# First network of a two layer transformer: two buffers for the transposed input, the next batch turned ahead of the sixth gate and up pair, and sums awaited bank by bank

## The reference

```
logits = x @ W_router                                   # 8 experts
scores = sigmoid(logits); top 2 of scores + expert_bias, their scores normalised -> w
gate   = x @ W_gate + lora(x, sA_gate, sB_gate) + sum_e w_e * lora(x, A_gate[e], B_gate[e])
up     = x @ W_up   + lora(x, sA_up,   sB_up)   + sum_e w_e * lora(x, A_up[e],   B_up[e])
hidden = silu(gate) * up                                # 688 columns
out    = hidden @ W_down + lora(hidden, sA_down, sB_down) + sum_e w_e * lora(hidden, A_down[e], B_down[e])
```

## Time and profile before

| | |
|---|---|
| time, median of 3 runs | 1555.84 us (1554.02 to 1556.76) |
| profiled execution, time | 1562.64 us |
| profiled execution, span | 1560.8 us |
| PE busy | 1425.5 us, 91% of the span |
| DVE, ACT, POOL busy | 60%, 37%, 35% |
| granted TensorE clock, mean | 0.960 |
| first network, from the first turn of `x1` to the last sum | 655.5 to 871.1 us |

### The profile page before, as it was taken

How to read it: one execution, slowest core, us unless ns; L and a number is a source line. 1 busy time by engine, 2 the same in 40 slices (tenths; PEclk the granted TensorE clock), 3 DMA queues, 4 the chain that set the end, 5 groups by cost and what they waited for, 6 DMA issues and landing times.

```text
span 1560.8 us, 23982 instructions
## 1 busy us (share of the span) xinstructions
PE 1425.5 (91%) x8106; PEld 1133.1 (73%) x8106; DVE 941.5 (60%) x2170; ACT 569.9 (37%) x1441; POOL 553.6 (35%) x483
## 2 busy tenths in 40 slices
PE   7999999999999999899999699999999999575990
PEld 6777777777777777677676588788788788563650
DVE  4677777777777778534332456565665657464214
ACT  4444444444444444521211243333334333331320
POOL 3555555555555555001002213513532522103223
PEclk9999999999999999989989899999999999788996
DMA  5000000000002000200000020200200004925984
GB/s 172 1 11 1 11 0 10 7 3 7 3 7 63 0 0 1 74 7 0 1 0 0 0 75 8 62 22 14 68 7 13 7 15 124 280 95 158 275 232 121
DMA packets 68218, 76.35 MB, mean 49 GB/s; under 512 B 14205, under 2 KB 55445, under 8 KB 68149
## 3 DMA queue, kind: packets, MB, share of 16 engines
q1 hardware_dynamic: 56789, 58.49, 13.2%
q10 hardware_dynamic: 8288, 12.22, 2.6%
q0 software_dynamic: 3072, 4.72, 1.6%
HBM read 66.22 MB, written 9.21 MB: 48 GB/s over the span
## 4 chain that ended last, share of the span: by engine, by line
PE 81%; DVE 8%; POOL 3%; issue 3%; DMA 2%; ACT 2%; another core or an unknown queue 1%; POOLq 0%; ACTq 0%; DVEq 0%
PE ps L1612 39%; PE ps L1728 9%; PE ps L1713 7%; PE ps L1701 5%; PE ps L1758 4%; PE ps L1848 4%; PE ps L1706 2%; PE ps L2054 2%; PE ps L1925 1%; PE ps L2119 1%; PE ps L1915 1%; DMA sums_dram<-rows 1%; PE ps L2136 1%; PE ps L1730 1%; PE ps L1703 1%
## 5 line engine op out<-in xcount | busy, mean ns | idle before, releaser
L617 POOL TENSOR_TENSOR qk<-q,ksb 128x512 f32<-128x512 f32 x64 | 82.6, 1291 | 303.6 <-ACT q L841 214.2
L756 ACT ACTIVATE probs<-ps,nm 128x128 f32<-128x128 f32 (+3 forms) x256 | 134.0, 526 | 152.7 <-DVE nm L1116 152.7
L1728 PE MATMUL ps<-kT,qT 128*128 128x128 f32 (+3 forms) x512 | 174.6, 450 | 4.4 <-ACT probs L756 3.7
L1040 DVE TENSOR_TENSOR pT_low<-ps,pT 128x384 fp32r<-128x384 f32 (+2 forms) x256 | 99.7, 451 | 122.6 <-ACT pT L699 121.1
L1057 DVE TENSOR_TENSOR prod<-ps,rope_sb 128x1024 f32<-128x1024 f32 x128 | 150.2, 1215 | 6.4 <-PE ps L1612 6.4
L495 POOL TENSOR_TENSOR qT<-prod 64x512 f32<-64x512 f32 x64 | 81.3, 1270 | 170.2 <-DVE prod L1057 131.6
L699 ACT ACTIVATE pT<-ps 128x384 fp32r<-128x384 f32 (+2 forms) x256 | 84.9, 415 | 152.0 <-PE ps L1758 152.0
L1713 PE MATMUL ps<-U,oT 128*128 (+1 forms) x512 | 124.6, 386 | 0.7 <-ACT oT L699 0.7
L1116 DVE TENSOR_REDUCE nm<-ps 128x1 f32<-128x128 f32 (+3 forms) x256 | 113.7, 484 | 12.1 <-PE ps L1730 12.1
L495 POOL TENSOR_TENSOR kT<-prod 64x512 f32<-64x512 f32 x64 | 81.4, 1272 | 111.2 <-DVE prod L1057 108.7
L1166 DVE SCALAR_TENSOR_TENSOR acc<-ps,rinv,acc 128x256 f32<-128x256 f32 x256 | 109.5, 479 | 13.5 <-PE ps L1713 11.9
(11 more groups left out here) (256 smaller groups left out, 2763.1 us busy)
## 6 DMA issues: line engine op xcount, KB each, us to landing
eg<-in_L_ffn_w_gate_dram SPq DMA_DIRECT2D x16, 704.0 KB
eg<-in_L_ffn_w_up_dram SPq DMA_DIRECT2D x16, 704.0 KB
ed<-in_L_ffn_w_down_dram ACTq DMA_DIRECT2D x10, 640.0 KB
ksb<-ks_dram SPq DMA_DIRECT2D x16, 256.0 KB, 3.3
ed<-in_L_ffn_w_down_dram SPq DMA_DIRECT2D x6, 640.0 KB
rows_dram<-rows ACTq DMA_DIRECT2D x4, 640.0 KB, 3.3
acc<-in_L_attn_x_dram SPq DMA_DIRECT2D x4, 512.0 KB
wq_in<-in_L_attn_wq_dram SPq DMA_DIRECT2D x8, 256.0 KB, 2.8
```

The costliest lines, as they stand in the source:

```text
L617: nc.gpsimd.tensor_tensor(qk[:], q3[:], ksb[b % 2][:], ALU.mult).then_inc(qk_ready, 1)
L756: nc.scalar.activation(probs[hh][:, off:off + (i + 1) * P], ps[:, BS + i % 2, 0:(i + 1) * P], ACT.Exp, bias=nm[:, hh, i:i + 1], accum_out= ...
L1040: return nc.vector.tensor_tensor(o, whole, hi.bitcast(F32), ALU.subtract)
L1728: pe.matmul(ps[:, bank, 0:(i + 1) * P], qT[:, hh, b, i * P:(i + 1) * P], kT[:, hh, b, 0:(i + 1) * P], start=True, stop=False)
```

## The change

- `x1T` becomes two pairs of tiles, at 56 and at 102 KB of each partition; batch b uses pair `b % 2`.
- On PE, `turn_x1(b + 1)` is issued after the fifth pair (m = 4) and ahead of the sixth. `first_products(b + 1)` stays behind the sixth. On ACT `x1_halves(b + 1)` stands between the silus of m = 4 and m = 5, on DVE `x1_rests(b + 1)` between the products of m = 4 and m = 5.
- At the start of batch b, `base` waits ahead of each of its first four pieces for the sum of its own bank, in the order bank 0, 2, 1, 3 (the first, third, second and fourth sum), where it waited once for all four.
- The loops over batches are written out on PE, ACT and DVE (the tiles are chosen by `b % 2`); the constant `LINKS0` and the bookkeeping for the loop go.

```
--- before.py
+++ after.py
@@ -46,7 +46,6 @@
 PPC = 4
 BLOCKS = CHUNKS * BATCH
 
-LINKS0 = 39
 SCALE = float(DH) ** -0.5
 MASKED = -1.0e30
 ROPE_BASE = 10000.0
@@ -127,7 +126,7 @@
         gu = [place(f"gu{h}", 20 + 11 * h, [P, KD, 2, F0], F32R) for h in range(2)]
         lb = [place(f"lb{h}", 42 + 5.5 * h, [NL, 2, F0], F32R) for h in range(2)]
         la = [place(f"la{h}", 53 + 1.25 * h, [P, KD, NA], F32R) for h in range(2)]
-        x1T = [place(f"x1T{h}", 56 + 4 * h, [P, KD, T], F32R) for h in range(2)]
+        x1T = [[place(f"x1T{i}{h}", at + 4 * h, [P, KD, T], F32R) for h in range(2)] for i, at in enumerate((56, 102))]
         xaT = [place(f"xaT{h}", 64 + 4 * h, [NL, 2, T], F32R) for h in range(2)]
         gated = [place(f"gated{h}", 72 + 2 * h, [M0, T]) for h in range(2)]
         hidT = place("hidT", 76, [M0, FT0, T])
@@ -799,7 +798,7 @@
             def x1_halves(b):
                 for k in range(KD):
                     act.wait_ge(x1_turned, b * KD + (k + 1))
-                    copy(x1T[0][:, k, :], ps[:, 4 + k, :]).then_inc(x1hi_ready, 1)
+                    copy(x1T[b % 2][0][:, k, :], ps[:, 4 + k, :]).then_inc(x1hi_ready, 1)
 
             def scores0(b):
                 act.wait_ge(logits_ready, b + 1)
@@ -819,8 +818,9 @@
                     if m >= 2:
                         act.wait_ge(hid_ready, b * FT0 + (m - 1))
                     nc.scalar.activation(gated[m % 2][0:size, :], ps[0:size, m % 2, :], ACT.Silu).then_inc(gated_ready, 1)
+                    if m == 4 and not last:
+                        x1_halves(b + 1)
                 if not last:
-                    x1_halves(b + 1)
                     scores0(b + 1)
                     xa_halves(b + 1)
                 act.wait_ge(ha_turned, b + 1)
@@ -832,9 +832,8 @@
             x1_halves(0)
             scores0(0)
             xa_halves(0)
-            with act.Fori(0, BATCH - 1) as b:
-                ffn0(b, False)
-            ffn0(BATCH - 1, True)
+            for b in range(BATCH):
+                ffn0(b, b == BATCH - 1)
 
 
             def relu(o, i):
@@ -1191,7 +1190,7 @@
             def x1_rests(b):
                 for k in range(KD):
                     dve.wait_ge(x1hi_ready, b * KD + (k + 1))
-                    rest(x1T[1][:, k, :], ps[:, 4 + k, :], x1T[0][:, k, :]).then_inc(x1lo_ready, 1)
+                    rest(x1T[b % 2][1][:, k, :], ps[:, 4 + k, :], x1T[b % 2][0][:, k, :]).then_inc(x1lo_ready, 1)
 
             def route0(b):
 
@@ -1250,8 +1249,9 @@
                                             ALU.mult).then_inc(hid_ready, 1)
                     if m == 1 and not last:
                         norm1(b + 1)
+                    if m == 4 and not last:
+                        x1_rests(b + 1)
                 if not last:
-                    x1_rests(b + 1)
                     route0(b + 1)
                 for i in range(TPB):
                     dve.wait_ge(down_ready, b * TPB + (i + 1))
@@ -1281,15 +1281,8 @@
             route0(0)
             take_weights()
             xa_rests(0)
-            before = done[1]
-            done[0], done[1] = before, 0
-            ffn0(0, False)
-            with dve.Fori(1, BATCH - 1) as b:
-                done[0], done[1] = b * LINKS0 + before, 0
-                ffn0(b, False)
-                assert done[1] == LINKS0, done
-            done[0], done[1] = before + LINKS0 * (BATCH - 1), 0
-            ffn0(BATCH - 1, True)
+            for b in range(BATCH):
+                ffn0(b, b == BATCH - 1)
 
 
             def relu_rest(o, whole, hi):
@@ -1795,7 +1788,7 @@
                 for i in range(TPB):
                     for k in range(KD):
                         last = mm3(ps[:, 6 + i // 2, (i % 2) * NA:(i % 2 + 1) * NA],
-                                   lambda a: x1T[a][:, k, i * P:(i + 1) * P], lambda c: la[c][:, k, :], k == 0, k == KD - 1)
+                                   lambda a: x1T[b % 2][a][:, k, i * P:(i + 1) * P], lambda c: la[c][:, k, :], k == 0, k == KD - 1)
                 last.then_inc(logits_ready, 1)
 
             def turn_xa(b):
@@ -1813,7 +1806,7 @@
                     f, size = F0S[m]
                     for k in range(KD):
                         mm3(ps[0:size, 2 * w + m % 2, :], lambda a: gu[a][:, k, w, f:f + size],
-                            lambda c: x1T[c][:, k, :], k == 0, False)
+                            lambda c: x1T[b % 2][c][:, k, :], k == 0, False)
 
                 def lora(m, w):
                     f, size = F0S[m]
@@ -1822,11 +1815,11 @@
                     if w:
                         last.then_inc(gate_ready, 1)
 
-                if not first:
-
-                    pe.wait_ge(ffn_added, b * TPB)
                 for m in range(2):
                     for w in range(2):
+                        if not first:
+
+                            pe.wait_ge(ffn_added, (b - 1) * TPB + 2 * w + m + 1)
                         base(m, w)
                 if first:
                     turn_xa(0)
@@ -1839,8 +1832,9 @@
                             base(m, w)
                     for w in range(2):
                         lora(m, w)
+                    if m == 4 and not last_one:
+                        turn_x1(b + 1, False)
                 if not last_one:
-                    turn_x1(b + 1, False)
                     first_products(b + 1, False)
                 pe.wait_ge(hid_ready, b * FT0 + FT0)
                 for i in range(TPB):
@@ -1864,10 +1858,8 @@
             pe.wait_ge(w0_lo, 6)
             first_products(0, True)
             pe.wait_ge(dn_loaded, 13 * 16)
-            ffn0(0, True, False)
-            with pe.Fori(1, BATCH - 1) as b:
-                ffn0(b, False, False)
-            ffn0(BATCH - 1, False, True)
+            for b in range(BATCH):
+                ffn0(b, b == 0, b == BATCH - 1)
 
 
             def queries(u, b, i):
```

## The result

| | before | changed |
|---|---|---|
| median, us | 1555.19 (4 runs, 1554.02 to 1556.76) | 1538.34 (4 runs, 1532.52 to 1540.49) |
| ratio to before | | 0.988 (95% interval 0.9853 to 0.9908) |
| profiled execution: time, span | 1562.64, 1560.8 | 1537.87, 1536.1 |
| PE busy | 1425.5 | 1414.8 |
| mean granted clock | 0.960 | 0.967 |

What follows compares the result with a forecast made beforehand. PE, busy 91% of the span, was taken as the bound, losing time to 1.73 us waits for `x1T` and low clock behind them. 5.7 + 8.4 + 0.6 + 0.2 = 14.9 us off 1555.84 gave about 1541, range 1536 to 1550.

Steps and rivals of the forecast that it cites:

- Turn ahead of the sixth pair: Batches 0 to 2, ahead of the products with `la`: moving the turn saves 1.89 us each, 5.7 in all, lower bound 5.2.
- The covers: Slack hiding the moved work: 2.3 us for copies and rests, 7 for `x1s`, 1.5 for the last hidden piece.
- the wait only moves: Rival: PE meets rests, last hidden piece or first silu later, clock falls as before; 1553 to 1556 us, chance 0.04.
- Clock: Products with `la` and down products of batches 1 and 2 regain full clock: 8.4 us, bounds 0 and 15.
- Bank by bank: Batch borders, sums awaited separately: first silu comes 0.2 us earlier each, 0.6 in all, bounds 0 and 2.0.
- loops: Batch borders, loops written out: 0.1 us for each of two looped batches, 0.2 in all, bounds 0 and 0.5.
- Sum: Whole kernel: 5.7 + 8.4 + 0.6 + 0.2 = 14.9 us off the profiled 1562.64, so 1547.7.
- clock 1.00 to the end of batch 3: Sign expected in the profile after: granted clock 1.00 from about 685 us to the end of batch 3.
- Carrying the sum to the medians: Whole 14.9 us taken off the unprofiled median 1555.84, 6.8 below the profiled time, giving 1540.9, about 1541.
- only idle time: Rival: clock falls as before or timed runs lose less of it; gain only 6.5 us, time 1549.3, chance 0.18.
- Turn brings the clock down: Rival: transposes between pairs halve the clock from the sixth pair on, 9.2 us a batch; 1568.5 us, chance 0.05.
- the two readings in the prediction: Moved turn as a pause for the clock: enough by itself, 1568.5 us; or needing the wait too, 1541.

Runs made afterwards that it cites:

- e1: Changed kernel with the turn, ACT's copies and DVE's rests put back behind the sixth pair; 1550.40 us, ratio 0.9983 to the kernel before.
- e4: As e1, with 8 unused matmuls of 512 columns on PE between the turn and the products with `la`; 1543.62 us, ratio 0.994.
- e3: Kernel before with its loops over batches written out on PE, ACT and DVE, nothing else; 1552.80 us, ratio 0.9987.
- e9: Changed kernel with DVE making the rests of `x1T` behind the sixth hidden piece, so PE waits ahead of the products with `la`; 1552.04 us, ratio 1.0024.
- e2: Changed kernel with one wait for all four sums at the start of a batch; 1537.79 us, ratio 0.9901.
- e5: Changed kernel with the eight transposes of the moved turn done twice, 16 in a row; 1537.62 us, ratio 0.9928.
- e6: Changed kernel with ACT's next-sublayer copy moved behind the next batch's second silu, and POOL's normalisation root ahead of its work on that copy; 1542.50 us, ratio 0.9944.
- e7: As e6, with the down products started when five of six hidden pieces are there; 1537.45 us, ratio 0.993.
- e8: As e7, with POOL's work on the copied rows and weight halves held until DVE has written the third hidden piece; 1531.94 us, ratio 0.9889.

## Why the prediction was right

1541 us was forecast with 1536 to 1550; measured 1538.34. Its steps, from the profiles:

- **Turn ahead of the sixth pair, 5.7 us.** From the third pair to the products with `la` a batch took 748.13 - 728.55 = 19.58 us and takes 742.93 - 725.25 = 17.68: 1.90, where 1.89 was taken; 5.7 in three. The covers held: no wait for `x1T`, none for `x1s`, none for the last hidden piece. With them falls the rival that the wait only moves.
- **Clock, 8.4 us.** Products with `la` and down products of batches 1 and 2 fell by (4.15 - 2.80) + (5.35 - 2.81) + (15.58 - 13.46) + (16.02 - 13.46) = 8.6. That idle time is the cause was inferred in the prediction and is shown by e1 and e4 together. In the profiles with a hole ahead of these products (before, e1, e3, e9) 11 of 12 batches lost clock; in the nine others none of 27 did there.
- **Bank by bank, 0.6 us, and loops, 0.2.** 0.9 by e2 and 0.3 by e3, each alone; together 0.43 + 0.52 + 0.42 = 1.4 at the borders where 0.8 was taken. The mechanism is as written: the silu behind the table load, and a new wait of 0.44 to 0.45 us (0.5 was named). The size was short because the prediction held that nothing ahead of the table load would move. ACT's copy starts 7.17, 7.28 and 7.28 us after the `ldn` products before and 7.05 to 7.06 now, 0.12 at the first border, for which I had counted nothing, and 0.22 at the others, for which I had counted 0.1. E3 shows that this is the loops' part: with only the loops written out the copy starts at 7.06 too.
- **Sum.** 5.7 + 8.6 + 1.4 = 15.7 against 14.9. In the profiles the first network shrank by 15.2: the first pairs of batch 0 ran 1.3 us faster and batch 3's down products 1.7 slower, by the clock. Neither was forecast, and that they nearly cancel is luck. The sign "clock 1.00 to the end of batch 3" failed with the second: 0.90 from 836 to 853 us. The median moved 16.9 (14.3 to 22.9 by its interval).
- **Carrying the sum to the medians.** I could not say what the 6.8 us between profiled time and median were and feared clock in this stage. The stretches above put them in the last sublayer. E1 and e3 lost clock in three batches of three in their one profile each, which speaks against an excess in the profile of before, with two; the runs without a profile have no trace that could show it. The median moved by the whole sum and more, and e4, which pays for the hole but keeps its clock, is at 1543.62; so the rival of only idle time (1549.3) falls.
- **Turn brings the clock down** (0.05): the changed kernel's clock of 1.00 behind each moved turn refutes it, and e5 does with twice the transposes. The rule of the Trainium skill ("TensorE: Matmul & The Clock Gate", Part 4) that transposes do not count as work for the clock in the way of matmuls is not contradicted by that: of the two readings in the prediction, the one in which the pause alone is enough (1568.5) did not come true. Eight more transposes between dense pairs cost 0.88 us a batch and no clock.

## What to carry to other kernels

Price a wait of PE by the speed of what comes after it, too: here 2.0 us of hole cost 5.3 a batch, and useless matmuls in it won back 3.3. Not every such wait costs clock (seven of eleven did ahead of batch 3's down products, three of four ahead of the fifth pair in e6 and e7), so read several batches and profiles before putting a price on one. A wait taken from PE at the head of a chain that another engine sets (here ACT behind a copy and a table load) mostly reappears further on. When work on POOL is moved, look at what DVE does at that moment, even where neither waits for the other's result.

## What the hardware showed that I had not expected

- The loss of clock by the hole ahead of the products with `la` came in two sizes only. Over 2.81 and 13.46 us, products with `la` and down products together lost 3.4 to 3.5 us in eight batches (before, e1, e3, e9) and 5.1 in the three others, with holes of 1.73 and of 2.60 us alike. At other places it had other sizes: 1.7 us or nothing behind the 1.41 us ahead of batch 3's down products, and 1.5, 1.5, 2.4 and nothing behind the 2.85 us ahead of the fifth pair (e6, e7; 3.06 us at full clock). Wide matmuls behind a wait did not prevent a fall.
- Four scalings of 128x256 on DVE took 4.60 us beside a POOL subtraction of 2.40 us and the weight halves behind it, and 1.38 without them, while POOL's subtraction took 2.40 in both (e6, e8). DVE was held, not POOL. The Trainium skill, "SBUF — State Buffer" (section "SBUF: two separate sides"), says that the two share a port pair, which a POOL operation and a DVE operation in certain forms claim, and which the first to start keeps for its whole instruction. The trace agrees that one blocks and the other does not slow down: the first scaling took 2.55 us and ended 0.15 us after the subtraction. That is 2.1 of the 3.2 us lost; the other 1.1 were lost by the three scalings beside the weight halves. Whether DVE's scaling is of the form that claims the pair is not shown by any run here.
- The stretch of the last sublayer varied from 211.8 to 218.9 us between profiles, once 227.2. A gain of 3 us elsewhere in this kernel is below that in whole times and is seen only in its own stretch.
